# Second cross attention of a four-layer network: scores in one group, another order of the steps, the last normalisation on GpSimd

## What is computed

```python
def _layernorm(x, axis=-1, eps=1e-05):
    m = jnp.mean(x, axis=axis, keepdims=True)
    v = jnp.var(x, axis=axis, keepdims=True)
    return (x - m) / jnp.sqrt(v + eps)
...
x = x + _L1_xattn_ref(_layernorm(x, axis=-1), ctx_1024, ctx_1024, L1_xattn_Wq, L1_xattn_Wk, L1_xattn_Wv, L1_xattn_Wo)
x = x + _L1_ffn_ref(_layernorm(x, axis=-1), ...
```

## Time and profile before

| | |
|---|---|
| time, median of 3 runs | 4461.92 us (4461.86 to 4462.62) |
| the profiled execution | 4463.79 us |
| its span, first to last instruction | 4461.9 us |
| the phase in question | about 311 to 563 us of the span |
| granted TensorE clock, mean over the span | 0.964 of full |
| busy, share of the span | PE 93%, DVE 84%, ACT 81%, POOL 70% |

### The profile page before, as it was taken

The page is one execution under the profiler, slowest core; times in us unless marked ns, Lnnn a source line. Parts: engine busy times, 40 slices in busy tenths (PEclk is TensorE's granted clock), DMA queues, the critical chain, the costliest instruction groups (busy, mean ns, idle before and its releaser), DMA issues. The chain is left out here.

```text
span 4461.9 us, 151456 instructions
## 1 busy us (share of the span) xinstructions
PE 4151.8 (93%) x51003; PEld 2730.7 (61%) x51005; DVE 3759.0 (84%) x9029; ACT 3596.7 (81%) x12939; POOL 3144.2 (70%) x4201
## 2 busy tenths in 40 slices
PE   6949999999999999999999999999999999777885
PEld 3426656666666666666666666666666666445543
DVE  4779989888889889889889888889889886788497
ACT  6938868888888888888888888888888887688435
POOL 2522278888888888888788888888889886444262
PEclk8969999999999999999999999999999999899986
DMA  2000000000000000000000000000000000000000
GB/s 64 0 21 1 0 8 2 2 3 17 13 2 2 2 21 9 2 3 2 21 8 2 2 12 12 8 2 3 17 12 2 2 2 2 1 0 0 29 1 20
DMA packets 38631, 37.27 MB, mean 8 GB/s; under 512 B 11382, under 2 KB 30068, under 8 KB 37748
## 3 DMA queue, kind: packets, MB, share of 16 engines
q1 hardware_dynamic: 38004, 28.97, 2.3%
HBM read 26.86 MB, written 2.10 MB: 6 GB/s over the span
## 5 line engine op out<-in xcount | busy, mean ns | idle before, releaser
L2326 ACT ACTIVATE stack_prob<-ps,stack_shift_by 128x128 f32<-128x128 f32 x3072 | 1078.8, 377 | 2.3 <-DVE stack_shift_by L2448 1.7
L2254 POOL TENSOR_TENSOR stack_qk<-stack_qk,stack_rsin 128x512 f32<-128x512 f32 x768 | 968.8, 1272 | 42.5 <-DVE stack_rsin L2473 42.5
L2261 POOL TENSOR_TENSOR stack_qk<-stack_qk,stack_inv 128x512 f32<-128x512 f32 x768 | 793.3, 1044 | 221.8 <-ACT stack_inv L2345 221.8
L2646 PE MATMUL ps<-local_wqkv,stack_xsT 128*128 128x512 f32 x1536 | 799.9, 603 | 3.8 <-DVE stack_rsin L2473 2.0
L2268 POOL TENSOR_TENSOR stack_prob<-stack_prob,stack_rs 128x512 f32<-128x512 f32 x768 | 791.0, 1041 | 1.7 <-DVE stack_rs L2455 1.7
L2326 ACT ACTIVATION_READ_ACCUMULATOR stack_prob<-ps,stack_shift_by 128x1 f32 x3072 | 669.6, 218 | 1.4 <-issue 1.4
L2448 DVE TENSOR_REDUCE stack_shift_by<-ps 128x4 f32<-128x512 f32 x768 | 524.1, 682 | 77.4 <-PE ps L2725 72.5
L2473 DVE TENSOR_TENSOR stack_rsin<-ps,stack_sin_t 128x256 f32<-128x256 f32 x1536 | 572.0, 413 | 4.7 <-issue 4.7
L2462 DVE TENSOR_TENSOR stack_qk<-ps,stack_cos_t 128x512 f32<-128x512 f32 x768 | 525.3, 684 | 38.9 <-ACT stack_sq L2334 37.8
L2480 DVE TENSOR_REDUCE stack_ss<-stack_sq 128x8 f32<-128x512 f32 x768 | 513.5, 669 | 0.7 <-ACT stack_sq L2334 0.7
L2334 ACT ACTIVATE stack_sq<-ps 128x512 f32<-128x512 f32 x768 | 467.9, 609 | 57.0 <-PE ps L2646 49.9
(11 more groups left out here) (342 smaller groups left out, 8555.1 us busy)
## 6 DMA issues: line engine op xcount, KB each, us to landing
local_wqkv<-L_ffn_Wqkv SPq DMA_DIRECT2D x30, 256.0 KB, 2.7
local_wo<-L_ffn_Wo SPq DMA_DIRECT2D x6, 512.0 KB, 4.6
out<-quantised_res SPq DMA_DIRECT2D x8, 256.0 KB, 2.3
local_w<-L_ffn_W SPq DMA_DIRECT2D x6, 341.0 KB
local_wqkv<-L_ffn_Wqkv SPq DMA_DIRECT2D x1, 1536.0 KB, 6.2
early_L_decay<-c_decay SPq DMA_DIRECT2D x1, 1024.0 KB, 10.9
local_w<-L_ffn_W SPq DMA_DIRECT2D x12, 64.0 KB
load_raw<-L_ffn_w SPq DMA_DIRECT2D x8, 64.0 KB, 1.9
```

The lines of the kernel that those rows point to most:

```text
L2254: nc.gpsimd.tensor_tensor(qk[w][:, j, :, :], qk[w][:, j, :, :], rsin[j % 2][:, :, :], ALU.add).then_inc(rot_ready, 1)
L2261: nc.gpsimd.tensor_tensor(qk[w][:, j, :, :], qk[w][:, j, :, :], bcast(inv[:, w, 8 * j:8 * j + 8].unsqueeze(2), [P, 8, LH]), ALU.mult).then ...
L2326: last = nc.scalar.activation(prob[w][:, g, j, :], ps[:, 4 + g % 2, j * P:(j + 1) * P], ACT.Exp, bias=shift_by[:, w, h:h + 1], accum_out=s ...
L2646: nc.tensor.matmul(proj_bank(j), xsT[w][:, :], wqkv[:, 512 * j:512 * j + 512], start=True, stop=True).then_inc(proj_ready, 1)
```

## The change

It leaves the arithmetic as it is, but for the last normalisation, which becomes two instructions, and changes four things:

1. `scores` works out all four groups in one call, after one wait for all exponentials of the tile before.
2. `end_norm` goes from VectorE (one instruction) to GpSimd (a subtraction into a new tile `centred`, then a multiplication). `aggregate2` and `over_deviation2` get waits for it, since they write again what it reads.
3. ScalarE works out the first deviation six tiles ahead of its step (four before), in another place of its order.
4. The order of the steps, `lead` and `lag` are new on all four engines.

The diff, without the declarations of the new semaphore and tile:

```diff
@@ gpsimd
+            def end_norm(b, w, live):
+                if live(b):
+                    pool.wait_ge(moments2_ready, b + 1)
+                    nc.gpsimd.tensor_tensor(centred[:, w, :], tile_of(X, b), bcast(moments2[:, w, 0:1], [P, P]),
+                                            ALU.subtract).then_inc(centred_ready, 1)
+                    wait_alone(pool, env, rstd2_ready, b + 1)
+                    wait_alone(pool, env, centred_ready, b + 1)
+                    nc.gpsimd.tensor_tensor(tile_of(NORMED, b), centred[:, w, :], bcast(rstd2[:, w:w + 1], [P, P]),
+                                            ALU.mult).then_inc(xn2_ready, 1)
...
+                spread_heads(n + 1, v, live)
+                fetch_context(n + 2, u, live)
                 block_values(n, u, live)
-                fetch_context(n + 1, v, live)
-                spread_heads(n + 1, v, live)
-            sequence_loop(pool, NB, 1, 0, step)
+                end_norm(n - 3, v, live)
+            sequence_loop(pool, NB, 2, 3, step)
@@ scalar
             def over_deviation2(b, w, live):
                 if live(b):
+                    wait(act, xn2_ready, b - 1)
                     act.wait_ge(lnvar2_ready, b + 1)
...
-                evacuate_probs(n + 1, v, 1, live)
-                exponentials(n + 1, v, 3, live)
-                log_variance(n + 4, u, live)
-                over_deviation(n + 4, u, live)
-                log_variance2(n - 1, v, live)
-                evacuate_probs(n + 1, v, 2, live)
-                over_deviation2(n - 1, v, live)
                 exponentials(n + 2, u, 0, live)
                 exponentials(n + 2, u, 1, live)
                 exponentials(n + 2, u, 2, live)
                 evacuate_probs(n + 2, u, 0, live)
-            sequence_loop(act, NB, 4, 1, step)
+                exponentials(n + 2, u, 3, live)
+                evacuate_probs(n + 2, u, 1, live)
+                log_variance(n + 6, u, live)
+                evacuate_probs(n + 2, u, 2, live)
+                over_deviation(n + 6, u, live)
+                log_variance2(n, u, live)
+                over_deviation2(n, u, live)
+            sequence_loop(act, NB, 6, 0, step)
@@ vector
             def aggregate2(b, w, live):
                 if live(b):
-                    wait_alone(dve, env, stats2_ready, b + 1)
+                    waits_alone(dve, env, (stats2_ready, b + 1), (xn2_ready, b - 1))
...
-            sequence_loop(dve, NB, 2, 4, step)
+            sequence_loop(dve, NB, 3, 2, step)
@@ tensor
-            def scores(b, w, half, live):
+            def scores(b, w, live):
                 if live(b):
                     pe.wait_ge(spread_ready, b + 1)
                     pe.wait_ge(fixed_ready, b + 1)
-                    for g in (2 * half, 2 * half + 1):
-                        wait(pe, exp_ready, 4 * (b - 1) + g + 1)
+                    wait_alone(pe, env, exp_ready, 4 * b)
+                    for g in range(G):
                         r = slice(32 * g, 32 * g + 32)
                         nc.tensor.matmul(scores_of(g), fixed[r, w, :], spread[w][r, :, :], start=True,
                                          stop=True).then_inc(scores_ready, 1)
...
-            sequence_loop(pe, NB, 0, 3, step)
+            sequence_loop(pe, NB, 1, 2, step)
```

More of the change, by code:

```diff
@@ L632, in cross_attention_L1 @@
     xn2_ready = sem("xn2_ready")
+    centred_ready = sem("centred_ready")
+    centred = sb("centred", [P, 2, P])
     probT3_ready = sem("probT3_ready")
@@ L847, in step @@
                 maxima(n - 1, v, 2, live)
-                aggregate(n + 2, u, live)
-                evacuate_x(n, u, live)
+                evacuate_spread(n, u, live)
                 maxima(n - 1, v, 3, live)
+                evacuate_fixed(n, u, live)
+                evacuate_values(n, u, live)
                 one_over_rows(n - 2, u, live)
-                evacuate_spread(n, u, live)
                 evacuate_heads(n - 2, u, live)
-                evacuate_fixed(n, u, live)
-                end_norm(n - 4, u, live)
-                norm(n + 1, v, live)
-            sequence_loop(dve, NB, 2, 4, step)
+                statistics(n + 3, v, live)
+                aggregate(n + 3, v, live)
+                norm(n + 2, u, live)
+                residual(n - 2, u, live)
+                evacuate_x(n + 1, v, live)
+                statistics2(n - 2, u, live)
+                aggregate2(n - 2, u, live)
+            sequence_loop(dve, NB, 3, 2, step)
         @block.tensor
@@ L922, in step @@
                 v = 1 - u
-                output(n - 3, v, live)
-                turn_probs(n - 2, u, 2, live)
-                scores(n - 1, v, 0, live)
-                turn_x(n, u, live)
+                scores(n - 1, v, live)
                 turn_probs(n - 2, u, 3, live)
-                scores(n - 1, v, 1, live)
+                project(n, u, live)
                 weighted_values(n - 2, u, live)
-                project(n, u, live)
+                turn_x(n + 1, v, live)
                 turn_probs(n - 1, v, 0, live)
                 turn_probs(n - 1, v, 1, live)
-            sequence_loop(pe, NB, 0, 3, step)
+                output(n - 2, u, live)
+                turn_probs(n - 1, v, 2, live)
+            sequence_loop(pe, NB, 1, 2, step)
     ph.close(env)
```

## The result

The changed kernel took **4477.19 us** (median of 7 runs, 4470.18 to 4481.42) against 4461.92 us (median of 7, 4458.60 to 4463.51): a ratio of 1.0034, with a 95% interval of 1.0023 to 1.0046. It is slower, by 10 to 20 us. Forecast were 4467.9 us and a range of 4450 to 4478: the sign was right and the time lies in the range, at its upper end. The size was not right: +15.3 us came where +6.0 was forecast. The likeliest of the three cases had been a change within 0.2% (0.52); what came is the one that had 0.28.

The account below looks back on a forecast made before the run. TensorE was taken as full (199.43 of 200 us), at 7.37 us a tile; a new ring of 7.58 us gives 30 x 0.21 = +6.3, start −1.0, end +0.7: +6.0 us, median 4467.9 us, range 4450 to 4478.

Parts of the forecast that it names:

- The likeliest of the three cases: Whole program: a time within about 0.2%, 8.9 us, of the kernel before, chance 0.52; faster had 0.20, slower 0.28.
- The ring: Per tile: scores, VectorE's maxima and copies, turn_x, transposes, ScalarE's copy, fourth exponentials, back to scores: 7.58 us, 0.21 more.
- the signs named: Middle of phase: reciprocals 7.5 to 7.6 us apart, TensorE under 90% busy, its waits 0.4 and 0.7, ScalarE waits, L763 longer.
- the long end of the hand-overs: In the ring, three uncertain hand-overs between engines, taken as 0.12 us each; all at 0.18 give 7.76 us a tile.
- The sum: Whole phase: 30 x 0.21 = +6.3, start −1.0, end +0.7, together +6.0 us.
- Start: Phase start at 1.2 GHz: one score group goes, half of it returns as waiting: −1.0 us (0 to −2.1).
- End: Phase end: GpSimd's semaphore clears, now behind the last normalisation, delay the next phase; less L834, +0.7 us.
- an allowance for tiles at the lower clock: Upper end of the range, 4478 us: some seven tiles of the phase at the lower clock.
- What was hidden: Other work on all engines fits into waits; GpSimd's two products 0.26 us each, delay of L763 within VectorE's 1 us.
- the gain arrives: Rival: turn_x's wait is not last, the next ring decides, 7.03 us a tile, 4451.4 us in all; chance 0.21.
- the clock falls: Rival: TensorE's waits lower its clock, 1.5 us more on a ring; 10 of 30 tiles give +15, 4483; chance 0.14.
- The row of the load phase: Load phase, against the clock rival: TensorE did nothing but transposes there, with a granted clock of 1.00.

Follow-up runs that it names:

- the second executions: The kernel before and the changed kernel each run once more, unaltered: ratios 1.0001 and 1.0046 against the kernel before, phases 253.2 and 264.3 us.
- halves: Changed kernel with scores back in two groups of two products, the fourth transposes between them: 7.87 us a tile, ratio 1.0042 against the kernel before.
- vals_early: Changed kernel with VectorE's copies of keys, queries and values ahead of the fourth maxima: 7.16 us a tile, ratio 0.9986 against the kernel before.
- turn_later: Changed kernel with turn_x on TensorE moved behind the first two groups of transposed probabilities: 7.10 us a tile, ratio 0.9988 against the kernel before.
- norm_back: Changed kernel with turn_x behind two groups of transposes, GpSimd's clears before its loop, last normalisation back on VectorE ahead of the norm: 10.2 us a tile, ratio 1.0158.
- copy_on_vector: Changed kernel, turn_x later, clears first, VectorE making ScalarE's first copy of transposed probabilities, third transposes behind the scores: 7.38 us a tile, ratio 0.9993.
- merge_alone: Kernel before with only the four score products merged, in the second group's place behind the fourth transposes: 8.77 us a tile, ratio 1.0081.
- halves_output_later: Changed kernel with scores in two groups and the last product (output) behind the third group of transposes: 7.82 us a tile, ratio 1.0030.

## Why the prediction was right, and where it was off

- **The ring.** Named rightly, link by link: the values' copy binds `turn_x`, VectorE has no gap before it, the fourth exponentials release the scores. TensorE waits 0.48 us before `turn_x` (0.4 forecast) and 0.47 before the scores (0.7). Two of the signs named were off: the spacing (7.5 to 7.6) was 7.71 over the 30, and ScalarE's wait before its second group of exponentials is only 0.04 us.
- **Its length.** 7.58 us forecast, 7.76 measured in the middle. That the long end of the hand-overs also gave 7.76 is a coincidence: the three that were priced at 0.12 are 0.15, 0.14 and 0.08 us, 0.37 together where 0.36 was forecast. Mean of 24 turns, forecast in brackets: VectorE 3.68 (3.67), to `turn_x` 0.15 (0.12), to the next transposes 0.21 (0.16), from there to ScalarE's copy 0.73 (0.63), copy 0.49 (0.48), exponentials 1.14 (1.14), to the scores 0.14 (0.12), to the maxima 1.22 (1.26). The term that was mis-sized is the one priced from the earlier trace rows as "turn_x 0.16, the first transposes 0.60 to their end, hand-over to ScalarE 0.03"; it makes 0.15 of the 0.18 us. The trace divides it. `turn_x` takes 0.05 and the four transposes (0.65) another 0.05 more than in the kernel before. In halves, which has the same instructions there and a TensorE that had not waited, they take 0.17 and 0.60 as forecast; in vals_early, without a wait right before them either, 0.17 and 0.64, so what makes the transposes longer is open. The hand-over is 0.04 us in one step and 0.12 in the next, alternately; in the long one ScalarE's queue has one more register instruction between the end of the transposes and the copy (line 47, the helper `wait`; at 432.82 for instance).
- **The sum.** 30 spacings: +10.2 us instead of +6.3. Start: the first reciprocal is 1.2 us earlier, and 1.0 in the second executions (−1.0 forecast). End: +0.57 (+0.7), the clears being half hidden. Together +9.6, for +6.0. The medians are 15.3 us apart, and 4477.19 is beyond 4474.3, the long end of the forecast's own sum. That it still lies in the range is luck: the range reaches it by an allowance for tiles at the lower clock, and no tile of the profiled middles ran so; the 5 us beyond the phase have no term in the forecast.
- **What was hidden** stayed so. VectorE still waits 1.03 to 1.11 us before the first maxima. GpSimd's two products take 0.40 us each, not 0.26, and the norm 0.43 at the median instead of 0.33; both disappear in that wait:

```profile
L777 DVE TENSOR_SCALAR L_cross_xn<-X,L_cross_moments,L_cross_rstd x32: 317/426/556, 313.4 to 541.4; 128x128 f32 x24, 128x128 f32<-128x128 f32 x8
```

- **The rival "the gain arrives"** was priced at 7.03 us a tile and 10.5 us saved, if `turn_x`'s wait were not the last to end. turn_later is that case: 7.10 us, 10.2 us of the phase. The ring that then decides is the one written down (mean of 23 turns, forecast in brackets): to the end of the second maxima 1.89 (1.91), to the second group of exponentials 0.11 (0.12), two groups 2.03 (2.0), copy 0.49 (0.48), fourth group 1.17 (1.14), to the scores 0.19 (0.12), to the maxima 1.22 (1.26).
- **The rival "the clock falls"** did not occur: 1.00 in both executions, with waits of about 0.5 us. By the rule cited for it (no full clock for transposes; the Trainium skill, "TensorE: Matmul & The Clock Gate", section "Part 4: PE-mode transpose") it was likely; the trace does not agree. The row of the load phase that the forecast set against that rule shows less than it seems to: the profile gives 1.00 also for the 5.29 us before it, and for the first 10 us, in which TensorE did nothing.

```profile
24.91:30.20 5.29, 5.29 (x25) 5.29 (x26) 0.00 (x0) 3.87 (x20) 0.00 (x0) 1.00 0.55 154
```

The pace is what speaks there: up to 30.2 us the transposes start 0.21 us apart, behind it 0.11, which is their pace in the phase at 1.00. So the full clock came while TensorE did nothing but transposes. But norm_back shows that such a fall is near; the last section has its rows.

## What to carry to other kernels

Relieving the fullest engine pays only if no ring of waits is almost as long: add the ring up from start to start before counting busy time. An instruction that waits for a shared bank belongs behind the instructions that the ring needs; here an instruction of 0.16 us in the wrong place, with its wait, turned a gain of 10 us of the phase into a loss of 10. A ring or a queue that is added up from busy times alone comes out short: here by 0.46 us a tile in copy_on_vector. And here an instruction that a neighbouring engine locked out handed its place to the next one when it was moved away.

## What was not expected of the hardware

The granted clock can fall where the busy share does not tell it. norm_back and merge_alone keep TensorE busy for the same share of 200 us, at 0.89 and at 1.00:

```profile
340.00:540.00 200.00, 152.39 (x1936) 115.53 (x1929) 132.76 (x360) 129.12 (x456) 37.41 (x120) 0.89 0.00 0
```

```profile
340.00:540.00 200.00, 151.66 (x2231) 111.51 (x2223) 160.17 (x412) 150.27 (x526) 44.51 (x138) 1.00 0.00 0
```

On norm_back's TensorE there are two waits close together in each tile, of 0.9 to 1.0 and 0.7 to 1.2 us, and in 13 of 20 tiles the weighted values behind them run at the lower level (1.2 GHz), in the others not. The length of a wait alone does not tell it: merge_alone has one of 1.50 us before the weighted values of each tile, and one of 0.64 before `turn_x`. Two tiles of norm_back:

```profile
359.40 0.49 PE L877 MATMUL ps<-L_cross_xnT,L1WqT 128*128 128x128 f32 x2 [0.86 <-DVE L_cross_xnT L772]
...
361.30 1.94 PE L913 MATMUL ps<-L_cross_probT,L_cross_vbd 128*32 128x128 f32 x32 [0.97 <-issue]
362.98 1.82 PE L913 MATMUL ps<-L_cross_probT,ones_bd 128*32 128x128 f32 x32
...
369.93 0.49 PE L877 MATMUL ps<-L_cross_xnT,L1WqT 128*128 128x128 f32 x2 [1.01 <-DVE L_cross_xnT L772]
...
371.78 1.08 PE L913 MATMUL ps<-L_cross_probT,L_cross_vbd 128*32 128x128 f32 x32 [0.91 <-issue]
372.65 1.08 PE L913 MATMUL ps<-L_cross_probT,ones_bd 128*32 128x128 f32 x32
```

They take 3.44 us there (361.30 to 364.74, when the next instruction starts) and 1.89 here (371.78 to 373.67), 1.5 us of a tile, after waits of nearly the same length. What decides between the two was not tested.

At the start of the phase, too, the clock rises earlier in one execution than in another. halves and halves_output_later differ there in nothing but the place of one product (and ran on different chips); their stretches of 311 to 320 and 320 to 340 us are

```profile
311.00:320.00 9.00, 6.01 (x22) 3.64 (x22) 4.97 (x19) 2.66 (x12) 1.47 (x3) 0.51 0.67 223
320.00:340.00 20.00, 17.66 (x130) 10.87 (x128) 11.56 (x30) 13.36 (x46) 3.82 (x12) 0.74 0.00 1
```

```profile
311.00:320.00 9.00, 6.38 (x29) 3.84 (x28) 5.57 (x18) 4.08 (x15) 3.23 (x8) 0.65 0.35 116
320.00:340.00 20.00, 18.98 (x217) 12.39 (x216) 15.29 (x38) 16.76 (x59) 3.76 (x12) 1.00 0.01 2
```

and the first reciprocal came 24.4 and 19.7 us after the phase's first instruction. A term of 1 us at a phase's start, as in the forecast, is less than that difference, though the two pairs of executions of the kernels before and after agree on it.
